# Flamingo block with four gated layers on one core: the last stage's token rows in fixed regions per expert, routed and sent group by group beside the attention

## The chip, the cores and the metric

One NeuronCore of a Trainium2 chip runs the whole block in one launch. The metric is the device time of that launch in microseconds (us), float32 in and out.

## What is computed

x is 2 x 1024 tokens of 256 values, the context 2 x 154 rows of 256. Four layers follow each other, each an attention on the context and a feed-forward part, all gated by tanh and added to x. Cut to the part that matters:

```python
x = x + tanh(g_ffn[2])   * L2_ffn(layernorm(x))               # 8 experts, the best one per token, 256 -> 1024 -> 256
x = x + tanh(g_xattn[3]) * L3_xattn(layernorm(x), ctx, ctx)   # single head, quantised weights, softmax over 154
x = x + tanh(g_ffn[3])   * L3_ffn(layernorm(x))

def L3_ffn(x, router_w, router_bias, gate_w, up_w, down_w, sgate_w, sup_w, sdown_w):
    scores = softmax(x @ router_w.T + router_bias)            # 32 experts
    topk_scores, topk_idx = top_k(scores, 4)
    topk_scores = topk_scores / topk_scores.sum(-1)
    h = silu(einsum('nd,ehd->neh', x, gate_w)) * einsum('nd,ehd->neh', x, up_w)
    sel = take(einsum('neh,edh->ned', h, down_w), topk_idx)
    out = (sel * topk_scores[..., None]).sum(1)
    return out + silu(x @ sgate_w.T) * (x @ sup_w.T) @ sdown_w.T   # the shared expert, 512 wide
```

## The kernel before

Tokens lie on the 128 partitions, 16 tiles of 128 (T), in four groups of four tiles (G = 4, GT = 4). Each engine has one program written out in order; they meet at semaphores. The stages are numbered 0 to 7: even ones are the attentions, odd ones the feed-forward parts. The change touches three of them and the filling of a buffer at the start.

Stage 5 (the 8 experts): the router gives each token a slot in a buffer xs5 in HBM, sorted by expert and padded to whole tiles of 128 (NT2 = 24 tiles). POOL scatters the 16 tiles of rows with indirect DMAs (scatter_gpsimd), the tile loop (expert_tiles_tensor, _scalar, _vector, _sync) loads a tile, multiplies it with its expert's weights and stores it to ys5 in the same order, and after the loop POOL gathers 16 tiles back with indirect DMAs (gather_gpsimd, L1130). combine_parts (L1138) adds a group to x_tok and starts its layer norm.

Stage 6 (single head): single_context_* turns the context into keys and values (L1150 to L1216). single_* then walks the four groups: ScalarE normalises (L1424), PE transposes (L1413), ScalarE copies (L1419), PE makes scores (L1229), VectorE adds the bias and takes the maximum, ScalarE takes the exponential, PE transposes it (L1244, L1249), ScalarE and VectorE (L1311) copy it, PE multiplies with the values (L1257, L1258), VectorE adds to x_tok (L1318). The scores of group g + 1 are made ahead of the rest of group g; a norm's small steps (L1344 to L1382) are put between other work of VectorE.

Stage 7: when all groups are through stage 6, route_tensor, route_scalar and route_vector take them one by one: norm, transposes, logits (L573), top 8 and their index (L614, L617), a 0/1 mark per expert (L621, L628), running sums over the tiles (L634). When all 16 tiles are marked, PE counts ranks (L580, L582), VectorE turns counts into tiles per expert and start tiles (L640 to L651), and a slot is start * 128 + rank (L655 to L663). shares_vector makes the four weights of each token. POOL then sends 64 tiles of rows (16 tiles x 4 choices, 268 values a row: the token and 12 extras) to xs7 (L686), a buffer of 96 tiles sorted by expert. Meanwhile shared_* computes the shared expert for three of the groups: per group four hidden steps of eight matmuls (L717, ScalarE's tanh L747, VectorE's L761 and L765), and an output of 32 matmuls (L727) with its addition (L755). quads_* then handles the 96 tiles four at a time, 24 quads: SP loads a quad (L774), PE transposes (L809), multiplies (L816, L833), VectorE selects the token and weight of each row, and POOL sends the rows to ys7 (L955). The last group of the shared expert and the combination (L965) follow.

The order inside the shared expert and the waits of its first step:

```python
pe.wait_ge(*slots_ready.at(7, 1))
pe.wait_ge(*expert_ready.at(7, 1))
pe.wait_ge(*logits_read.at(7, G))
for k in range(4 * groups[0], 4 * groups[-1] + 4):
    hidden(k)
    if k % 4 == 0 and k // 4 - 1 in groups:
        down(k // 4 - 1)
```

SP fills xs5 and xs7 with zeros at the start (L2427, L2429), after the loads of stages 0 to 3 and ahead of those of stage 2's attention, which wait for stage 0.

## Time and profile before

| | us |
|---|---|
| median of 3 runs (lowest, highest) | 1704.92 (1700.68, 1713.27) |
| the profiled execution | 1705.23 |
| its span, first to last instruction | 1703.5 |

| engine | busy us | share of the span |
|---|---|---|
| PE matmul | 1372.4 | 81% |
| PE weight load | 769.7 | 45% |
| VectorE | 755.6 | 44% |
| ScalarE | 439.3 | 26% |
| GpSimd (POOL) | 287.6 | 17% |

The engines' times are those of one profiled execution; PE is TensorE, DVE is VectorE, ACT is ScalarE, SP is SyncE, a name with q is an engine's instruction queue. A line L765 is line 765 of the kernel. In a row of the timeline stand start, length, engine, line, operation, output and inputs, the number of instructions, and in brackets how long the engine had been idle and what ended that. TensorE's granted clock is given as a share of full speed: 1.0 is the 2.4 GHz level, 0.5 the 1.2 GHz level.

### The profile page before, as it was taken

The page shows a single profiled execution, that of the slowest core. Times are in us where ns is not written, and L with a number is a line of the kernel's source. Part 1 is how long each engine was busy: PE and PEld are TensorE (multiplying, and loading weights), DVE is VectorE, ACT ScalarE, POOL GpSimd, SP SyncE. Part 2 cuts the span into 40 slices and gives each one's busy share as a digit, 9 for nine tenths or more (in the row PEclk, how much of TensorE's full clock was granted, in tenths as well). Part 3 has the DMA queues.
Part 4 walks back from the last instruction along what each step waited for, and adds up shares of the span by engine and source line. Part 5 has one row for each costly group of instructions (what it writes and reads, how often), then busy time and mean ns, then how long its engine had stood idle before and what let it go on. Part 6 is the DMA issues. An engine that isn't in the chain of part 4 may idle for free.

```text
span 1703.5 us, 18737 instructions
## 1 busy us (share of the span) xinstructions
PE 1372.4 (81%) x6041; PEld 769.7 (45%) x6042; DVE 755.6 (44%) x2011; ACT 439.3 (26%) x837; POOL 287.6 (17%) x300
## 2 busy tenths in 40 slices
PE   5999999999736799999988299997578605888883
PEld 3433334334323344444445267765346303677762
DVE  6363472381476235555644112212545402345446
ACT  2212212121142234444433033331223000223220
POOL 2200110010022000000000300002300472154550
PEclk9899999999967689999988599998765757999997
DMA  9600000000010000000003901111072131144436
GB/s 323 208 1 0 0 0 0 0 0 0 1 50 1 1 1 1 1 1 1 27 1 122 331 28 31 32 36 57 25 243 92 62 110 61 52 142 136 134 112 252
DMA packets 82953, 113.86 MB, mean 67 GB/s; under 512 B 7376, under 2 KB 71504, under 8 KB 82768
## 3 DMA queue, kind: packets, MB, share of 16 engines
q1 hardware_dynamic: 73680, 87.54, 15.9%
q0 software_dynamic: 9216, 25.57, 4.2%
q8 instruction: 34, 0.56, 0.1%
q14 instruction: 23, 0.19, 0.0%
HBM read 68.07 MB, written 45.02 MB: 66 GB/s over the span
## 4 chain that ended last, share of the span: by engine, by line
PE 70%; DVE 12%; issue 8%; ACT 4%; another core or an unknown queue 2%; DMA 1%; POOL 1%; SPq 1%; DVEq 0%; ACTq 0%; POOLq 0%
PE psum L1605 16%; PE psum L816 5%; PE psum L1030 5%; PE psum L1014 5%; PE psum L1773 5%; PE psum L717 4%; PE psum L1829 2%; DVE arena L2343 2%; PE psum L1759 2%; PE psum L1806 2%; PE psum L573 2%; PE psum L1562 2%; PE psum L1853 2%; PE psum L1596 2%
## 5 line engine op out<-in xcount | busy, mean ns | idle before, releaser
L1605 PE MATMUL psum<-arena 128*128 128x512 f32 (+1 forms) x576 | 294.0, 639 | 0.3
L1605 PEld LDWEIGHTS psum<-arena 128*128 128x128 f32 (+1 forms) x576 | 96.9, 193 | 165.1 <-issue 162.4
L2343 DVE TENSOR_REDUCE arena<-psum 128x4 f32<-128x616 f32 x128 | 102.0, 797 | 127.3 <-PE psum L1773 126.0
L1773 PE MATMUL psum<-arena 32*128 32x308 f32 x512 | 112.7, 519 | 24.2 <-DVE arena L2343 22.9
L955 POOL DMA_INDIRECT ys<-xnT,arena x96 | 92.2, 961 | 151.5 <-DVE xnT L921 128.2
L1939 ACT ACTIVATE arena<-psum,arena 128x512 f32<-128x512 f32 x72 | 49.1, 686 | 234.1 <-PE psum L1605 224.8
L816 PE MATMUL psum<-arena,xn 128*128 x384 | 89.2, 385 | 24.3 <-ACT xn L866 13.4
L2053 ACT ACTIVATE arena<-psum 128x2048 f32<-128x2048 f32 x40 | 75.0, 1875 | 76.7 <-PE psum L1810 59.7
L1030 PE MATMUL psum<-arena,xn 128*128 x384 | 88.6, 385 | 2.0 <-ACT xn L1076 2.0
L1014 PE MATMUL psum<-arena,side 128*128 x192 | 88.5, 604 | 1.0 <-ACT side L1069 0.6
L816 PEld LDWEIGHTS psum<-arena,xn 128*128 128x128 f32 x384 | 71.0, 190 | 38.5 <-issue 29.8
L717 PE MATMUL psum<-xnT,side 128*128 128x512 f32 x64 | 35.1, 710 | 65.4 <-issue 62.5
L1773 PEld LDWEIGHTS psum<-arena 32*128 32x128 f32 x512 | 42.2, 201 | 92.4 <-DVE arena L2343 61.3
L1095 DVE COPY xn<-psum 128x1024 f32<-128x1024 f32 x24 | 29.4, 1225 | 119.3 <-PE psum L1014 119.3
L1443 POOL TENSOR_TENSOR arena<-arena 128x1024 f32<-128x1024 f32 x15 | 28.3, 1893 | 298.3 <-DVE arena L2192 279.0
L686 POOL DMA_INDIRECT xs<-xn,arena x64 | 61.5, 961 | 101.7 <-DVE xn L707 82.5
L1030 PEld LDWEIGHTS psum<-arena,xn 128*128 128x128 f32 x384 | 72.3, 193 | 11.9 <-issue 2.8
L1512 POOL TENSOR_TENSOR x_tok<-x_tok,add_row 128x1024 f32<-128x1024 f32 x16 | 37.7, 2364 | 228.6 <-ACT xn L1424 157.1
L1076 ACT ACTIVATE xn<-psum,side 128x128 f32<-128x128 f32 x192 | 52.3, 384 | 86.8 <-PE psum L1023 86.8
L2176 DVE SCALAR_TENSOR_TENSOR arena<-arena 128x512 f32<-128x512 f32 x24 | 16.5, 688 | 117.3 <-ACT arena L1939 117.3
L1806 PE MATMUL psum<-arena 32*128 32x512 f32 x256 | 53.2, 667 | 1.9 <-ACT arena L2053 1.9
L717 PEld LDWEIGHTS psum<-xnT,side 128*128 128x128 f32 x64 | 14.4, 231 | 84.8 <-issue 81.1
(374 smaller groups left out, 2207.9 us busy)
## 6 DMA issues: line engine op xcount, KB each, us to landing
arena<-in_W SPq DMA_DIRECT2D x16, 1024.0 KB
xs<-zeros SPq DMA_DIRECT2D x1, 12864.0 KB, 53.9
xn<-xs SPq DMA_DIRECT2D x24, 536.0 KB
arena<-in_gate_up SPq DMA_DIRECT2D x4, 2048.0 KB, 15.0
arena<-ys SPq DMA_DIRECT2D x4, 2048.0 KB, 14.7
arena<-in_down SPq DMA_DIRECT2D x4, 1024.0 KB, 14.9
xs<-zeros SPq DMA_DIRECT2D x1, 3072.0 KB, 15.3
side<-xs SPq DMA_DIRECT2D x24, 128.0 KB
```

The source lines that it names most:

```text
L686: pool.indirect_dma_start(xs, bass.IndirectOffsetOnAxis(r["slot_i"][:, n, k:k + 1].bitcast(U32), 0), xn[:, n // GT, n % GT, 0:xs.shape[1]] ...
L717: ins = pe.matmul(bank[2 * (k % 2) + j], w[:, c, h * P:(h + 1) * P], place(7, g)[:, c], start=(c == 0), stop=(c == C - 1))
L816: ins = pe.matmul(bank[2 + t // 2][:, (t % 2) * 2 * F4:(t % 2 + 1) * 2 * F4], qinT[:, u, c, t * P:(t + 1) * P], arena[:, bass.ds(e * (C * ...
L955: pool.indirect_dma_start(ys7, bass.IndirectOffsetOnAxis(row_i[:, u, t:t + 1].bitcast(U32), 0), qout[:, u, t * D:(t + 1) * D], None).then_ ...
L1014: ins = pe.matmul(bank[2 + h], xinT[:, u, c * P:(c + 1) * P], W1[:, e, c * F2 + h * 512:c * F2 + h * 512 + 512] if isinstance(e, int) else ...
L1030: ins = pe.matmul(bank[6 + u][:, 0:D], hact[:, u, k * P:(k + 1) * P], arena[:, bass.ds(e * (8 * D) + (E2 * C * F2 + k * D), D)], start=(k ...
L1076: ins = act.activation(hact[:, u, k * P:(k + 1) * P], bank[4 + k // 4][:, k % 4 * P:(k % 4 + 1) * P], ACT.Relu, bias=b1col[:, bass.ds(e * ...
L1605: ins = pe.matmul(bank[dict(hn=4, r=5, z=6, xn=7)[k]][:], lhs[:, cols], r, start=(start and n == 0), stop=(stop and n == len(w) - 1))
L1773: ins = pe.matmul(bank[4 + i][:, 0:2 * M].rearrange("p (h m) -> p h m", h=2), qhT[rows, n % 3, c, t * P:(t + 1) * P], keys[rows, l, c, b, ...
L1806: pe.matmul(bank[j], keys[rows, l, r // 2, b, r % 2, 0:P], qhT[rows, n % 3, r // 2], start=True, stop=False, tile_position=(32 * j, 0))
L2053: act.activation(e_rest if r == 4 else e_head[:, r % 2], psum[:, 0:4], ACT.Exp, scale=HD ** -0.5).then_inc(weighed, 1)
L2343: dve.tensor_reduce(neg[:, n % 2, t, 2 * pair:2 * pair + 2, 2 * c:2 * c + 2], psum[:, 4:6, 0:2 * M].rearrange("p b (h m) -> p b h m", h=2) ...
```

## The change

1. xs7 becomes a region of 16 tiles for each of the 32 experts, and one spare tile of zeros: 513 tiles in place of 96, filled with zeros at the start in nine DMAs. A slot is expert * 2048 + rank, which needs no counts of the other groups. rows_vector works out, for the 96 tiles of the quad loop, the first row of each in the regions; SP reads it and loads each of a quad's four tiles by a DMA of its own.
2. Routing goes by groups: while group g is in stage 6, group g - 1 gets its norm, transposes (turn_late, copy_late), logits, marks (hot_vector), ranks and slots (slots_vector), and POOL scatters its 16 tiles of rows (scatter7_gpsimd). Group 3 follows inside the shared expert, by the functions in `then`, as do counts and tiles per expert. The shared expert no longer waits for all slots but for those of three groups.
3. Buffers move for it: the transposed groups 1 and 2 lie in the last quarter of the down weights' place, so that quarter (1 MB) is loaded after the twelfth hidden step. The router's weights are loaded with stage 5's.
4. Stage 5: rows carry their slot and token number, the tile loop's output goes to HBM in token order by one indirect DMA a tile (scatter_out5_gpsimd), with a selection on VectorE (select), and four plain loads (combined5_sync) take the place of the 16 gathers.

The core of the diff:

```diff
+REGION = T
+SPARE = E4 * REGION
...
-        tanh_s = xq[:].rearrange("p u n -> p (u n)").bitcast(F32).rearrange("p (u n) -> p u n", u=2)
...
+        tanh_s = arena[:, 28672:29696].rearrange("p (u n) -> p u n", u=2)
+        xnT7 = [xq[:].rearrange("p u n -> p (u n)").bitcast(F32).rearrange("p (c n) -> p c n", c=C)] + [
+            region.rearrange("p (c n) -> p c n", c=C)
+            for region in (arena[:, TAIL - 2048:TAIL - 1024], arena[:, TAIL - 1024:TAIL], side[:, 3200:4224])]
...
-        ys5 = nc.dram_tensor("ys5", (NT2 * P, D), F32, kind="Internal").ap()
-        xs7 = nc.dram_tensor("xs7", (NT4 * P, DX), F32, kind="Internal").ap()
+        xs5 = nc.dram_tensor("xs5", (NT2 * P, D5), F32, kind="Internal").ap()
+        ys5 = nc.dram_tensor("ys5", (1 + T * P + NT2 * P, D), F32, kind="Internal").ap()
+        xs7 = nc.dram_tensor("xs7", ((SPARE + 1) * P, DX), F32, kind="Internal").ap()
...
+        def turn_late(pe, s, g):
+            i, b = late_turns[s, g], late_bank(s, g)
+            pe.wait_ge(*xn_ready.at(s, g + 1))
+            for c in range(C):
+                if b == 0 and i:
+                    pe.wait_ge(*xnT_ready.at(6, (i - 1) * C + c + 1))
+                for t in range(GT):
+                    ins = pe.transpose(bank[b + c][:, t * P:(t + 1) * P], xn[:, g, t, c * P:(c + 1) * P], ident[:])
+                ins.then_inc(turned.sem, 1)
+        def copy_late(act, s, g):
+            i, b = late_turns[s, g], late_bank(s, g)
+            for c in range(C):
+                act.wait_ge(*turned.at(6, i * C + c + 1))
+                act.activation(place(s, g)[:, c], bank[b + c][:], ACT.Copy).then_inc(xnT_ready.sem, 1)
...
+        def logits_tensor(pe, g):
+            pe.wait_ge(wr7_loaded, 2 * 16)
+            pe.wait_ge(*xnT_ready.at(6, (late_turns[7, g] + 1) * C))
+            for t in range(GT):
+                for c in range(C):
+                    ins = pe.matmul(logit_bank[:, t * E4:(t + 1) * E4], place(7, g)[:, c, t * P:(t + 1) * P], wr7[:, c],
+                                    start=(c == 0), stop=(c == C - 1))
+            ins.then_inc(logits_done.sem, 1)
+        def ranks_tensor(pe, g):
+            r = route[7]
+            pe.wait_ge(*hot_ready.at(7, g + 1))
+            pe.wait_ge(*earlier_ready.at(7, 1 + GT * (g + 1)))
+            if g == G - 1:
+                pe.matmul(bank[5][0:E4, 128:129], r["earlier"][:, T], ones_bf[:, 0:1], start=True, stop=True)
+            for t in range(GT):
+                dst = rank_bank[:, t * E4:(t + 1) * E4]
+                pe.matmul(dst, before[:], r["any_hot"][:, t], start=True, stop=False)
+                ins = pe.matmul(dst, ones_bf[:], r["earlier"][:, g * GT + t], start=False, stop=True)
+            ins.then_inc(ranks_done.sem, 1)
...
+        def hot_vector(dve, ch, g):
+            r = route[7]
+            if g == 0:
+                dve.wait_ge(route_consts, 7)
+                dve.memset(r["earlier"][:, 0], 0.0).then_inc(earlier_ready.sem, 1)
+            dve.wait_ge(*logits_done.at(7, g + 1))
+            dve.tensor_tensor(r["logits"], logit_bank.rearrange("p (t e) -> p t e", t=GT),
+                              br7.unsqueeze(1).broadcast_to([P, GT, E4]), ALU.add).then_inc(logits_read.sem, 1)
+            dve.wait_ge(*logits_read.at(7, g + 1))
+            for t in range(GT):
+                ch.step(dve.max(r["top"][:, t], r["logits"][:, t]))
+            ch.settle()
+            for t in range(GT):
+                ch.step(dve.max_index(r["index"][:, t], r["top"][:, t], r["logits"][:, t]))
+            if g:
+                dve.wait_ge(shares_exp, g)
+            dve.tensor_tensor(r["share"], r["top"][:, :, 0:K4], r["top"][:, :, 0:1].broadcast_to([P, GT, K4]),
+                              ALU.subtract).then_inc(shares_shifted, 1)
+            ch.settle()
+            ch.step(dve.tensor_copy(r["index_f"], r["index"][:, :, 0:K4]))
+            ch.settle()
+            if g:
+                dve.wait_ge(*ranks_done.at(7, g))
+            ch.step(dve.tensor_tensor(r["hot"].rearrange("p t k e -> p (t k) e"),
+                                      iota_e[:].unsqueeze(1).broadcast_to([P, GT * K4, E4]),
+                                      r["index_f"].rearrange("p t k -> p (t k)").unsqueeze(2).broadcast_to([P, GT * K4, E4]),
+                                      ALU.is_equal))
+            ch.settle()
+            with nc.allow_low_precision(reason="sums of zeros and ones"):
+                dve.tensor_reduce(r["any_hot"], r["hot"].rearrange("p t k e -> p t e k"), AX.X, ALU.add).then_inc(hot_ready.sem, 1)
+            dve.wait_ge(*hot_ready.at(7, g + 1))
+            for t in range(GT):
+                n = g * GT + t
+                dve.wait_ge(*earlier_ready.at(7, n + 1))
+                dve.tensor_tensor(r["earlier"][:, n + 1], r["earlier"][:, n], r["any_hot"][:, t],
+                                  ALU.add).then_inc(earlier_ready.sem, 1)
...
+        def slots_vector(dve, ch, g):
+            r = route[7]
+            dve.wait_ge(shares_exp, g + 1)
+            ch.step(dve.tensor_reduce(r["total"], r["share"], AX.X, ALU.add))
+            ch.settle()
+            ch.step(dve.reciprocal(r["total"], r["total"]))
+            ch.settle()
+            ch.step(dve.tensor_scalar(r["total"], r["total"], gain(7), None, ALU.mult))
+            ch.settle()
+            ch.step(dve.tensor_tensor(xn[:, g, :, D + K4:D + 2 * K4], r["share"],
+                                      r["total"].unsqueeze(2).broadcast_to([P, GT, K4]), ALU.mult))
+            dve.wait_ge(*ranks_done.at(7, g + 1))
+            ch.step(dve.scalar_tensor_tensor(r["place"], iota_e[:].unsqueeze(1).broadcast_to([P, GT, E4]), float(REGION * P),
+                                             rank_bank.rearrange("p (t e) -> p t e", t=GT), ALU.mult, ALU.add))
+            slot = r["slot"][:, g * GT:(g + 1) * GT]
+            for k in range(0, K4, 2):
+                ch.settle()
+                ch.step(dve.tensor_tensor(r["picked"], r["hot"][:, :, k:k + 2],
+                                          r["place"].unsqueeze(2).broadcast_to([P, GT, 2, E4]), ALU.mult))
+                ch.settle()
+                ch.step(dve.tensor_reduce(slot[:, :, k:k + 2], r["picked"], AX.X, ALU.add))
+            ch.settle()
+            ch.step(dve.tensor_copy(xn[:, g, :, D:D + K4], slot))
+            ch.settle()
+            dve.tensor_copy(r["slot_i"][:, g * GT:(g + 1) * GT], slot).then_inc(slots_ready.sem, 1)
...
+        def rows_vector(dve, ch):
+            r = route[7]
+            dve.wait_ge(*expert_done.at(7, 1))
+            ch.step(dve.tensor_tensor(rowid, bank[5][:, 256:256 + NT4], iota_n[:, 0:NT4], ALU.add))
+            ch.step(dve.tensor_scalar(r["expert_f"][0:1], bank[4][0:1, 256:256 + NT4], float(E4 - 1), None, ALU.min))
+            ch.settle()
+            ch.step(dve.tensor_scalar(rowid, rowid, float(SPARE), float(P), ALU.min, ALU.mult))
+            quad = r["expert_f"][0:1].rearrange("p (q t) -> p q t", t=4)
+            for t in range(2, -1, -1):
+                ch.step(dve.scalar_tensor_tensor(quad[:, :, t], quad[:, :, t + 1], float(E4), quad[:, :, t], ALU.mult, ALU.add))
+                ch.settle()
+            ch.step(dve.tensor_copy(first_row[0:1], rowid[0:1]))
+            ch.step(dve.tensor_copy(r["expert"][0:1, 0:NQ], quad[:, :, 0]))
+            ch.settle()
+            dve.tensor_scalar(rowid, rowid, pcol[:], None, ALU.add).then_inc(expert_ready.sem, 1)
...
+        def scatter7_gpsimd(pool, g):
+            pool.wait_ge(*slots_ready.at(7, g + 1))
+            for t in range(GT):
+                n = g * GT + t
+                for k in range(K4):
+                    pool.indirect_dma_start(xs7, bass.IndirectOffsetOnAxis(r7["slot_i"][:, n, k:k + 1].bitcast(U32), 0),
+                                            xn[:, g, t], None).then_inc(scattered.sem, 16)
...
-            pe.wait_ge(*expert_ready.at(7, 1))
-            pe.wait_ge(*logits_read.at(7, G))
+            pe.wait_ge(ws_loaded, 3 * 16)
+            pe.wait_ge(*xnT_ready.at(6, (late_turns[7, G - 1]) * C))
+            pe.wait_ge(scores_read6, 2 * G)
+            pe.wait_ge(*logits_read.at(7, G - 1))
+            pe.wait_ge(*slots_ready.at(7, G - 1))
             for k in range(4 * groups[0], 4 * groups[-1] + 4):
                 hidden(k)
+                if k in then:
+                    then[k]()
...
             def load(q, u):
-                sp.dma_start(qin[:, u], xs7[bass.ds(q * 4 * P, 4 * P), :].rearrange("(t p) d -> p t d", p=P)
-                             ).then_inc(in_loaded[u].sem, 16)
+                for t in range(4):
+                    row = sp.value_load(first_row[0:1, bass.ds(4 * q + t, 1)], min_val=0, max_val=SPARE * P)
+                    sp.dma_start(qin[:, u, t], xs7[bass.ds(row, P), :]).then_inc(in_loaded[u].sem, 16)
+            sp.wait_ge(*expert_ready.at(7, 1))
             sp.wait_ge(*scattered.at(7, T * K4 * 16))
             load(0, 0)
             load(1, 1)
+            sp.wait_ge(shared_done, 4 * (G - 1))
+            sp.dma_start(DW[:, 24:32], d["down"][24 * F4:32 * F4].rearrange("(e p) n -> p e n", p=P)).then_inc(w7_loaded, 16)
...
+        def combined5_sync(sp):
+            for u in range(2):
+                sp.wait_ge(*sent[u].at(5, NT2 // 2 * 16))
+            for g in range(G):
+                sp.dma_start(gathered5[:, g * GT:(g + 1) * GT],
+                             ys5[1 + g * GN:1 + (g + 1) * GN].rearrange("(t p) d -> p t d", p=P)).then_inc(gathered_in[g].sem, 16)
...
+            def select(i, u, turn):
+                one = slice(i, i + 1) if isinstance(i, int) else bass.ds(i, 1)
+                if not isinstance(turn, int) or turn:
+                    dve.wait_ge(*out_ready.at(5, i - 1))
+                dve.wait_ge(*in_loaded[u].at(5, 16 * turn + 16))
+                dve.scalar_tensor_tensor(token_row5[:, u:u + 1], xin[:, u, D:D + 1], rowid5[:, one], xin[:, u, D + 1:D + 2],
+                                         ALU.is_equal, ALU.mult).then_inc(chosen.sem, 1)
+                dve.wait_ge(*chosen.at(5, i + 1))
+                dve.scalar_tensor_tensor(no_token5[:, u:u + 1], token_row5[:, u:u + 1], 0.0, unused_row5[:, one],
+                                         ALU.is_equal, ALU.mult).then_inc(selected5, 1)
...
-            for n in range(T):
-                pool.indirect_dma_start(gathered5[:, n], None, ys5,
-                                        bass.IndirectOffsetOnAxis(route[5]["slot_i"][:, n, 0:1].bitcast(U32), 0)
-                                        ).then_inc(gathered5_in[n // GT], 16)
+        def scatter_out5_gpsimd(pool):
+            for i in range(NT2):
+                u = i % 2
+                pool.wait_ge(*out_ready.at(5, i + 1))
+                pool.indirect_dma_start(ys5, bass.IndirectOffsetOnAxis(row_i5[:, u:u + 1].bitcast(U32), 0), yout[:, u],
+                                        None).then_inc(sent[u].sem, 16)
...
+                if g:
+                    turn_late(pe, 7, g - 1)
                 pe.wait_ge(main_copied6, g + 1)
                 pe.wait_ge(rest_copied6, g + 1)
+                if g:
+                    logits_tensor(pe, g - 1)
                 if g:
                     pe.wait_ge(*x_done.at(6, g))
                 for t in range(GT):
                     ins = pe.matmul(dst, probs6R[0:MR, u, t * P:(t + 1) * P], vals6R[0:MR, b], start=False, stop=True)
                     if t % 2:
                         ins.then_inc(pv_done6, 1)
+                if g:
+                    ranks_tensor(pe, g - 1)
...
+                if g:
+                    normalise_scalar(act, 7, g - 1)
                 act.wait_ge(turned6, 2 * g + 1)
                 if g >= 2:
                     act.wait_ge(pv_done6, 2 * (g - 1))
                 act.activation(probs6T[:, u], bank[4], ACT.Copy).then_inc(main_copied6, 1)
+                if g:
+                    copy_late(act, 7, g - 1)
+                    share_scalar(act, g - 1)
...
+                run(norm)
                 if g + 1 < G:
                     scores(g + 1)
-                run(finish(g), norm)
-                run(norm)
+                finishing = finish(g)
+                run(itertools.islice(finishing, 3))
+                if g:
+                    hot_vector(dve, ch, g - 1)
+                run(finishing)
+                if g:
+                    slots_vector(dve, ch, g - 1)
...
+                for n, first in enumerate(range(0, SPARE + 1, 64)):
+                    many = min(64, SPARE + 1 - first)
+                    sp.dma_start(xs7[first * P:(first + many) * P].rearrange("(t p) d -> p t d", p=P),
+                                 zeros[:].unsqueeze(1).broadcast_to([P, many, DX])).then_inc(zeroed, 16)
...
-                route_tensor(pe, 7, wr7, (ws_loaded, 5 * 16), free=lambda: pe.wait_ge(*x_done.at(6, G)))
-                shared_tensor(pe, range(G - 1))
+                shared_tensor(pe, range(G - 1), {
+                    1: lambda: (turn_late(pe, 7, G - 1), logits_tensor(pe, G - 1)),
+                    2: lambda: ranks_tensor(pe, G - 1),
+                    3: lambda: start_tensor(pe),
+                    4: lambda: tiles_tensor(pe)})
...
-                route_vector(dve, ch, 7, br7)
-                shares_vector(dve, ch)
-                shared_vector(dve, ch, range(G - 1))
+                shared_vector(dve, ch, range(G - 1), {
+                    1: lambda: (hot_vector(dve, ch, G - 1), slots_vector(dve, ch, G - 1), tiles_vector(dve, ch)),
+                    2: lambda: passed_vector(dve, ch),
+                    4: lambda: rows_vector(dve, ch)})
```

## Rows read from the trace of the kernel before

**Rows 1.** Busy time by stretches: window, length, busy us (count), granted clock, DMA share, GB/s.

```profile
80.00:484.00 404.00, 372.45 (x907) 141.74 (x905) 206.98 (x362) 80.55 (x124) 42.33 (x25) 0.95 0.00 0
...
1240.00:1295.00 55.00, 42.35 (x121) 25.53 (x121) 26.90 (x116) 13.19 (x39) 2.56 (x2) 0.59 0.82 259
...
1335.00:1464.00 129.00, 68.95 (x191) 38.36 (x192) 21.03 (x36) 7.31 (x13) 61.91 (x66) 0.74 0.22 77
...
1464.00:1656.00 192.00, 163.24 (x867) 139.37 (x865) 90.03 (x265) 54.24 (x96) 87.35 (x91) 1.00 0.39 125
```

**Rows 2.** The chain that ended last, from 1334 to 1465: start, us, what.

```profile
1334.80 20.07 PE psum L717 x40
...
1361.78 3.43 PE psum L717 x8
1365.21 55.09 issue
...
1457.30 7.17 PE psum L727 x32
```

**Rows 3.** Timeline around the stop in the shared expert.

```profile
1337.56 1.00 POOL L686 DMA_INDIRECT xs<-xn,arena  x1 [82.47 <-DVE xn L707]
...
1417.30 0.96 POOL L686 DMA_INDIRECT xs<-xn,arena  x1 [0.30 <-issue]
...
1419.56 0.69 DVE L765 SCALAR_TENSOR_TENSOR arena<-xq,psum 128x512 f32<-128x512 f32 x1 [63.33 <-remote]
```

**Rows 4.** Timeline at the end of stage 5's gathers.

```profile
1195.03 1.91 PE L1167 MATMUL psum<-arena,ctxT 128*26 128x256 f32 x8
...
1199.05 1.20 PE L1178 MATMUL psum<-arena 128*128 128x308 f32 x4
...
1199.53 0.95 POOL L1130 DMA_INDIRECT side<-ys,xq  x1 [0.30 <-issue]
...
1203.31 0.68 DVE L1211 COPY arena<-psum 26x512 f32<-26x512 f32 x1 [7.08 <-remote]
...
1205.08 1.65 DVE L1138 SCALAR_TENSOR_TENSOR x_tok<-side,tanh_g,x_tok 128x256 f32<-128x256 f32 x4
```

**Rows 5.** Timeline of the single-head attention, from its second group on.

```profile
1240.33 1.97 PE L1413 MATMUL psum<-ident,xn 128*128 128x128 f32 x8
...
1253.18 1.19 PE L1257 MATMUL psum<-arena 128*128 128x256 f32 x2 [4.51 <-issue]
...
1262.35 1.97 PE L1413 MATMUL psum<-ident,xn 128*128 128x128 f32 x8
...
1294.27 0.48 DVE L1318 SCALAR_TENSOR_TENSOR x_tok<-psum,arena,x_tok 128x256 f32<-128x256 f32 x1
...
1295.39 1.40 DVE L1365 BATCH_NORM_STATS2 stats<-x_tok 128x6 f32<-128x256 f32 x4
...
1296.12 0.60 ACT L1419 ACTIVATE xnT<-psum 128x512 f32<-128x512 f32 x1 [12.40 <-PE psum L1413]
...
1299.49 0.16 DVE L1382 COPY scale_ln<-nwt 128x4 f32<-128x4 f32 x1
```

**Rows 6.** Timeline of the routing: one group's logits and marks, and the slots.

```profile
1297.47 2.06 ACT L1424 ACTIVATE xn<-x_tok,shift_ln,scale_ln 128x256 f32<-128x256 f32 x4
...
1309.76 3.62 PE L573 MATMUL psum<-side,arena 128*128 128x32 f32 x16 [0.69 <-ACT arena L1419]
...
1313.42 0.29 DVE L610 TENSOR_TENSOR arena<-psum,side 128x128 f32<-128x128 f32 x1 [1.46 <-PE psum L573]
...
1317.01 1.01 DVE L634 TENSOR_TENSOR arena<-arena 128x32 bf16<-128x32 bf16 x4
...
1327.68 0.69 DVE L659 TENSOR_TENSOR arena<-arena 128x512 f32<-128x512 bf16 x1
```

**Rows 7.** DMA issues: what, queue, count, KB each, us to landing.

```profile
xs<-zeros SPq DMA_DIRECT2D x1, 12864.0 KB, 53.9
```

**Rows 8.** Timeline of one expert tile of stage 5, VectorE.

```profile
1093.89 1.23 DVE L1095 COPY xn<-psum 128x1024 f32<-128x1024 f32 x1 [3.78 <-PE psum L1014]
```

312 lines of the change are left out of this document (169 added, 143 removed).

## The prediction

> **What bounds the kernel now.** I read the page first (PE is busy for 81% of the span, but the slices show it at 7 and lower in the last third), then the busy time by stretches, then the chain that ended last, and last the timeline around each hole of the chain. The stretches [rows 1] are to be read by PE's busy time against their length and by the granted clock: the expert quads (1464 to 1656) run at clock 1.00 with PE busy 163 of 192 us, while the attention (1240 to 1295) was granted 0.59 and the 129 us from 1335 on have PE busy for only 69. The chain says what those 129 us are [rows 2]: 20 us of shared-expert matmuls, 55.1 us in which PE issues nothing, and the rest of the shared expert, which ends at 1457.30 + 7.17 = 1464.5. So about 170 us lie between the end of the single-head attention and the first quad, and the matmuls of three shared groups in them are 62 us of work (12 hidden steps of 3.43 and 3 outputs of about 6.9, at the 2.4 GHz level). That is what the change can take.
>
> Why PE stood still is in [rows 3]. POOL issues its 64 scatters from 1337.56 on, one each 1.266 us, the last at 1417.30. The output matmuls of the first shared group (L727) are through at 1361.78, where the chain goes on with a hidden step [rows 2]; VectorE's L765, which waits only for them, starts at 1419.56, 57.8 us later and 1.3 us after the last scatter's issue. The same is seen once more, smaller, in the gathers of stage 5 [rows 4]: L1167 ends at 1196.94, VectorE's L1211 starts at 1203.31, 2.8 us after the last gather's issue ended. So a long run of indirect DMAs held back what PE had finished, in both runs that lie over working engines, and not before some 12 of them were out (the 16 gathers began 15 steps of 1.266 before 1199.53, at 1180.5). The rows call the releaser remote; the cause they don't show.
>
> **Stage 5 and the zeroing: near nothing.** The fill of the row buffer for the last stage grows from 96 to 513 tiles. The 12,864 KB took 53.9 us [rows 7], so 513 tiles take 288 us; begun within the first 20 us it is done by 310, and no DMA ran from 80 to 484 (share 0.00) [rows 1]; SP has nothing to load before. Priced at 0; were that cover gone, the attention weights of stage 2, next in SP's queue, would wait for the excess. In the 24 expert tiles SP loses its stores, POOL gains one indirect DMA a tile (1.27 of 8 us), VectorE two one-column operations and an add, 0.5 us together; VectorE idles 3.78 us in each tile before L1095 alone [rows 8], so these are hidden. SP's load now also waits for the selection two tiles back, over 11 us ahead of its use. The 16 gathers, 20 us of POOL, become four plain loads, and with them goes the hold at 1196.9 [rows 4]. VectorE would go on with L1211 at 1197.0 and, after PE's L1178 (ends 1200.3), reach its first combination at 1200.9 in place of 1205.08: **-4.2 us**.
>
> **Single-head attention: longer.** Groups 0 to 2 of the routing move in here. Per group PE gets 8 transposes (1.97 us), 16 logit matmuls (3.62) and 8 small rank matmuls (0.3), ScalarE a normalisation of 2.06 and two copies of 0.60 (1.3), VectorE the top-k part (L610 at 1313.42 to the last running sum at 1318.02: 4.6, with the share's subtraction 4.8) and the slots (four share operations 1.07, place 0.3, four operations at half the 512 elements of L659, 1.6, two copies 0.4: 3.4) [rows 5, 6]. All of it is at the 1.2 GHz level, as the stretch was granted 0.59 [rows 1]. The period of group 1 was 1240.33 to 1262.35. PE waited in it until 1253.18 for VectorE's copy; the transposes fit there, the logits come behind: **+3.6**. In groups 2 and 3 the new order makes one chain: last addition 0.9, slots of the group before 3.4, its norm 4.2 (1295.39 to 1299.65), ScalarE 2.1, transposes 2.0, copies 1.3, logits 3.6, the PV matmuls 9.2 (1253.18 to 1262.35): 26.7. Twice that, 53.4, stands in place of 31.2 (1262.35 to the end of the last PV matmul at 1293.5, just ahead of the last additions): **+22.2** [rows 5]. Bounds: if the fuller PE is granted 2.4 GHz, PV and logits halve and some 15 us come back; nothing lower.
>
> **Routing gap: gone but for one group's slots.** From VectorE's last addition (ends 1294.75) to the first shared matmul (1334.80) were 40.0 us; now PE waits for the slots of group 2, 3.4: **-36.6** [rows 2, 5].
>
> **Shared expert.** Its three groups take 61.9 us of PE. Put between them are group 3's transposes and logits (2.8 at the fast level), and PE waits where VectorE does routing: for ScalarE's copies 1.4, for the top-k before the ranks 2.2, for the tile counts and the next product 3.5, before the last output 2.1 as before: 9.2. Together 73.9, in place of 129.3 (1334.80 to 1464.1): **-55.4**. POOL's last burst starts some 20 us into this stage and takes 16 x 1.266 = 20.2, so the rows are all out by 42, with 32 us to spare before the first quad. The last quarter of the down weights, 1 MB, is now loaded after the twelfth hidden step, under an output of 6.9 and a wait of 2.1; at the zeroing's rate (12,864 KB in 53.9 us [rows 7]) it takes 4.3 us, so 5 to 7 with its start. Quads: four loads of a quad in place of one; SP issues one in about 0.5 us and has 7.9 per quad, priced 0. Tail unchanged.
>
> Sum: -4.2 + 3.6 + 22.2 - 36.6 - 55.4 = -70.4. The profiled execution took 1705.23 (span 1703.5), the median is 1704.92, so one stands for the other: 1634.5 without any hold.
>
> **The holds.** The 64 scatters now come in four bursts of 20.2 us, three with PE and VectorE handing work to each other and the third and fourth nearly back to back. What the trace bounds: nothing (as in the quads, where four DMAs in 7.9 us hold nobody for long), or all of every burst, 81 us. It is nearest to the gathers, also 16 DMAs: onset 16.3 us after the first, 6.4 us late in all. Four times that is 25; about half falls where VectorE isn't waited for. I take **+12**, and forecast **1646**.
>
> The Trainium skill ("SBUF — State Buffer", Who interferes with whom) has only one place where VectorE and GpSimd get into each other's way, a port pair that VectorE takes for operations with two SBUF inputs or in a two-port mode. L765 and L1211 read PSUM and at most one SBUF operand, so by that rule they would never be held and the time would be 1634; the row of 57.8 us speaks against it, and the measurement decides.
>
> **Rivals.**
> A, no hold, perhaps with PE at the higher clock in the attention: 1634, down to 1619. For it: bursts are 16 long, onset came after 12 or more. Against: 2 of 2 long runs held.
> B, the bursts hold much more: from the middle of each burst to its end and 2.8 us on, 13 us x 4 = 52: 1686. For it: in the long run the hold covered 58 of 82 us. Against: the gathers' 6.4.
> C, slower than before: each burst holds PE's results for its whole length, so that burst, selection and the next burst follow in series: 4 x 20.2 = 81 on 1634 gives 1715. It decides from 17.6 us held per burst on. Against it: 12 scatters went by without delay in both runs [rows 3, 4].
> D, the change doesn't do its main thing: the quads don't start when the shared groups end, because the weights' last quarter or the four loads are late. Each would cost at most its own length, 7 us, and 1 us per quad if the loads took over 7.9 us of SP: 1634 + 7 + 24 = 1665. The issues of 0.5 us speak against it.
>
> **How the numbers follow.** Forecast (holds of 5 to 25 in all) 0.5, A 0.18, B 0.17, C 0.07, D 0.08. The range leaves out C and the ends of A and B: 1618 to 1692. A measurement of this kernel tells about 1% from no change; faster than 1688 is the forecast, A, D and most of B, 0.85; within 1% the rest of B and part of C, 0.08; slower 0.07.
>
> **What would show it.** The first shared matmul (L717 before) near 1319 in place of 1334.8; the first quad near 1393 to 1405 in place of 1464; no PE gap over 20 us between them; the attention at 105 us in place of 84, clock still near 0.6; the four bursts of 16 apart by more than their length except the last two; a zeroing that ends near 310. Wrong would be: a VectorE wait with remote as releaser in each burst (B, C), a quad period over 8 us (D), or a slot iteration longer than its 130 us while the zeroing runs.

## The result, and the profile after

| | before | changed |
|---|---|---|
| median of 4 runs (lowest, highest), us | 1706.79 (1700.68, 1713.27) | 1653.06 (1651.77, 1657.03) |
| profiled span, us | 1703.5 | 1655.1 |

The ratio is 0.9694, with a 95% interval of 0.9664 to 0.9725: 3.1% faster. Forecast were 1646 and a range of 1618 to 1692. The spans differ by 48.4 us, the medians by 53.7; the profiled execution is the slowest of its four (1657.03).

The working below goes by stretches between the starts of certain instructions in the timelines, since these can be told in every variant:

| stretch, us | before | changed |
|---|---|---|
| last output matmul of stage 5 to VectorE's first combination (L1138, now L1328) | 28.0 | 22.8 |
| to the first score matmul of stage 6 (L1229, now L1419) | 10.8 | 10.9 |
| attention and routing: to the first shared matmul (L717, now L878) | 118.9 | 110.9 |
| shared expert: to the first quad's matmul (L816, now L990) | 131.5 | 93.2 |
| quads: to the last hidden matmul of the last quad | 181.9 | 185.5 |
| tail | 55.4 | 55.4 |

Up to the end of stage 5 the two are 0.6 us apart. Busy time by stretches of the changed kernel, columns as in [rows 1]:

```profile
1234.60:1321.00 86.40, 59.63 (x217) 40.46 (x216) 51.45 (x217) 20.99 (x56) 33.25 (x34) 0.56 0.60 203
...
1321.00:1414.00 93.00, 76.25 (x236) 43.83 (x236) 34.08 (x100) 11.26 (x21) 30.92 (x33) 0.88 0.22 71
...
1414.00:1600.00 186.00, 159.11 (x837) 136.49 (x838) 84.77 (x252) 51.50 (x93) 82.42 (x86) 0.99 0.42 125
```

The shared stretch has 76 us of PE's work in 93, where [rows 1] had 69 in 129. The chain that ended last says where the other 17 are (start, us, what); "another core or an unknown queue" is its name for a wait whose releaser the profile doesn't show (the timeline's "remote"); no other core runs here:

```profile
1321.04 9.34 PE psum L878 x16
...
1332.44 9.80 another core or an unknown queue
1342.26 0.29 DVE arena L645
...
1358.78 12.46 another core or an unknown queue
1371.26 0.70 DVE arena L933
1371.96 0.04 issue
1372.01 12.26 PE psum L878 x24
1384.27 6.91 PE psum L888 x32
...
1403.61 8.86 PE psum L888 x32
...
1414.26 1.77 PE psum L990 x7
```

The 55.1 us of [rows 2] have become two holes of 9.8 and 12.5. The timeline shows that they are of the kind of [rows 3]:

```profile
1199.33 1.26 DVE L1328 SCALAR_TENSOR_TENSOR x_tok<-side,tanh_g,x_tok 128x256 f32<-128x256 f32 x3
...
1287.81 1.66 DVE L1523 SCALAR_TENSOR_TENSOR x_tok<-psum,arena,x_tok 128x256 f32<-128x256 f32 x4 [3.50 <-remote]
...
1332.23 1.84 PE L606 MATMUL psum<-side 128*128 128x32 f32 x15
...
1340.11 0.96 POOL L868 DMA_INDIRECT xs<-xn,arena  x1 [0.30 <-issue]
1342.26 0.29 DVE L645 TENSOR_TENSOR arena<-psum,side 128x128 f32<-128x128 f32 x1 [9.82 <-remote]
...
1357.57 7.17 PE L888 MATMUL psum<-side,arena 128*128 128x256 f32 x32
...
1364.58 3.60 PE L878 MATMUL psum<-arena,side 128*128 128x512 f32 x8
...
1369.10 0.96 POOL L868 DMA_INDIRECT xs<-xn,arena  x1 [0.30 <-issue]
...
1371.26 0.69 DVE L933 SCALAR_TENSOR_TENSOR arena<-arena,psum 128x512 f32<-128x512 f32 x1 [12.54 <-remote]
```

POOL sends in four bursts of 16, from 1265.0, 1292.9, 1321.2 and 1350.1, one DMA each 1.265 us. VectorE's L645 waits for the logits (L606), through at 1334.1 and 13 us into the third burst; it starts at 1342.26, 8.2 us late and 1.2 us after the burst's last DMA. L933 waits for the output matmuls (L888), through at 1364.7, and starts 6.5 us late, again 1.2 us after the end of a burst. I call such a late start a hold. The first burst has two: L645 starts at 1278.5, 1.7 us after its matmuls and in the middle of the burst, and L1523 at 1287.8, 2.9 us after the last DMA. In the second burst no wait names remote. Two waits of the quads (who, for whom, us in all, times, longest):

```profile
ACT xn L1040 <- remote: 16.3, 12, 2.0
...
PE psum L983 <- DMA xn<-xs: 2.1, 1, 2.1
```

And the fill among the DMA issues, its eight large ones:

```profile
xs<-zeros SPq DMA_DIRECT2D x8, 8576.0 KB, 60.0
```

### The profile page after: what moved, and what is told of

Its sections match the earlier page's. It is cut to its first block, busy times and chain, and to the rows that moved or that the text cites. A ratio compares the mean times of both kernels' runs of the same rounds, so it can differ in the third digit from the quotient of the medians.

```text
span 1655.1 us, 19515 instructions
## 1 busy us (share of the span) xinstructions
PE 1370.3 (83%) x6042; PEld 768.6 (46%) x6043; DVE 774.8 (47%) x2121; ACT 438.6 (27%) x840; POOL 295.4 (18%) x310
## 4 chain that ended last, share of the span: by engine, by line
PE 69%; DVE 14%; issue 6%; ACT 5%; another core or an unknown queue 3%; DMA 2%; POOL 1%; SPq 1%; DVEq 0%; ACTq 0%; POOLq 0%
PE psum L1816 16%; PE psum L1201 5%; PE psum L1185 5%; PE psum L1984 5%; PE psum L990 5%; PE psum L878 3%; PE psum L2040 2%; DVE arena L2555 2%; PE psum L2017 2%; PE psum L1773 2%; PE psum L1970 2%; PE psum L2064 2%; PE psum L1807 2%; PE psum L888 1%
## 5 line engine op out<-in xcount | busy, mean ns | idle before, releaser
L1816 PE MATMUL psum<-arena 128*128 128x512 f32 (+1 forms) x576 | 289.3, 630 | 0.3
L990 PE MATMUL psum<-arena,xn 128*128 x384 | 89.1, 385 | 24.1 <-issue 13.1
L990 PEld LDWEIGHTS psum<-arena,xn 128*128 128x128 f32 x384 | 71.0, 190 | 38.1 <-issue 29.4
L1321 POOL DMA_INDIRECT ys<-side,xq x24 | 23.0, 959 | 183.8 <-DVE side L1284 183.8
L1069 DVE SCALAR_TENSOR_TENSOR arena<-arena,psum 128x512 f32<-128x512 f32 x24 | 16.5, 688 | 76.9 <-issue 50.0
```

The source lines that it names most:

```text
L990: ins = pe.matmul(bank[2 + t // 2][:, (t % 2) * 2 * F4:(t % 2 + 1) * 2 * F4], qinT[:, u, c, t * P:(t + 1) * P], arena[:, bass.ds(e * (C * ...
L1816: ins = pe.matmul(bank[dict(hn=4, r=5, z=6, xn=7)[k]][:], lhs[:, cols], r, start=(start and n == 0), stop=(stop and n == len(w) - 1))
```

## The experiments

Three theories: **S**, an unbroken run of POOL's indirect DMAs holds back what PE signals, until about a microsecond after the run (the first burst above doesn't fit this end); **F**, the delay is PE's own or belongs to these places in the code; **W**, there is no hold and the sum left out work. The kernels ran in three sets, each on a chip of its own; the kernel before took 1708.0 us on the first, 1708.7 on the second and 1666.8 on the third. Ratios are to the kernel before on the same chip. The changed kernel itself ran only in the first comparison (on which chip is not known) and not in these sets; its row below has the ratio of that comparison.

### First chip: does the hold go with the DMAs?

**One choice of four.** `for k in range(K4)` in POOL's burst becomes

```diff
-                for k in range(K4):
+                for k in range(1):
```

> The changed kernel with only the first of each token's four choices sent: four bursts of 4 indirect DMAs in place of four of 16. Left out: three quarters of the routed rows (their outputs are zeros; the row buffer of the outputs is zeroed at the start for that, 8 MB more under the first stage). All engine work, the number of expert tiles and every wait stay. Theory S (a long unbroken run of indirect DMAs on POOL holds back what PE signals; 4 in a row are too few): the holds seen in the changed kernel's trace (about 10 us in the third burst, 12.5 in the fourth, 2 to 4 in the first two) go, VectorE's waits with remote as releaser shrink below 2 us each, the shared stage is 74 to 78 us in place of 91, time 1629 to 1636. Theory F (PE's delay belongs to its own instruction stream or to these places in the code, not to the DMAs): the same holes at the same instructions, 1650 to 1655. Theory W (no hold; my sum for the shared stage left out real work or waits of the routing): 1648 to 1655, with the same 91 us.

**Paced by four.**

```diff
                 for k in range(K4):
                     pool.indirect_dma_start(xs7, ..., xn[:, g, t], None).then_inc(scattered.sem, 16)
+                pool.wait_ge(*scattered.at(7, (n + 1) * K4 * 16))
```

> The changed kernel with all 64 scatters, but POOL waits after every four until these have landed. Nothing is left out. Theory S (an unbroken run is what holds): each burst becomes four pieces of 5 us with gaps of 1 to 2 us, 26 to 30 us long; the last ends by about 1380, still ahead of the first quad; the holds go: 1630 to 1638, first quad at 1396 to 1400 in place of 1414. Rival Q (every indirect DMA of POOL costs PE's signals its share, however they are spaced): as much is held as before or more, since the bursts are longer: 1650 to 1660. Theory F (PE's own instruction stream): 1650 to 1655.

**Plain stores from SyncE.**

```diff
-                    pool.indirect_dma_start(xs7, bass.IndirectOffsetOnAxis(...), xn[:, g, t], None)
+                    sp.dma_start(xs7[(n * K4 + k) * P:(n * K4 + k + 1) * P, :], xn[:, n // GT, n % GT])
```

> The changed kernel with the 64 indirect scatters replaced by 64 plain stores of the same tiles (128 rows of 268 numbers) from SyncE's queue, after the same slots. Left out: the rows go to fixed places, so the experts see wrong rows (output buffer zeroed at the start as in the run with one choice); engine work and tile count stay. Theory S (it is POOL's indirect DMAs): no hold, 1629 to 1636. Rival D (it is the transfers' traffic, 137 KB each, whoever issues them): holds of the size seen before, 1645 to 1655. Theory F: 1650 to 1655.

**The kernel before, paced by four.** The same added line, in its one run of 64.

> The kernel before, with POOL waiting after every four of its 64 scatters of the last stage until they have landed. Nothing is left out. Theory S: VectorE's wait of 57.8 us at L765 goes, the three shared groups end near 1334.8 + 62 + 10 = 1407; the scatters take 81 + 16 x 1.5 to 2 = 105 to 113 us and end at 1443 to 1451, and they, not the shared expert, now set the first quad, at 1446 to 1454 in place of 1466: 1685 to 1694 in place of 1705. Theories F and Q (pacing changes nothing in what is held): the hold lasts as long as the scatters do, shared expert to about 1490, 1725 to 1735.

| | median us | ratio, 95% | attention | shared | quads |
|---|---|---|---|---|---|
| changed | 1653.1 | 0.969, 0.966 to 0.972 | 110.9 | 93.2 | 185.5 |
| one choice | 1645.4 | 0.964, 0.958 to 0.970 | 105.7 | 77.1 | 188.2 |
| paced by four | 1642.0 | 0.965, 0.959 to 0.971 | 105.8 | 77.2 | 186.7 |
| stores from SyncE | 1636.4 | 0.960, 0.956 to 0.964 | 105.8 | 77.0 | 186.0 |
| before, paced | 1693.0 | 0.991, 0.988 to 0.995 | 121.2 | 113.8 | 184.8 |

The two stages that the bursts lie over are alike in all three variants of the changed kernel, 5.1 and 16.1 us shorter than in the changed kernel itself. The engines' work and its order are unchanged in them, which speaks against F and W, and pacing sends all 64, which speaks against the rival by which every indirect DMA costs its share. It counts only if this chip holds at all, since the unpaced bursts were not run on it. That shows in the kernel before with its scatters paced (the gathers, left unpaced, below) and is settled on the second chip. The paced kernel's timeline at the place of the second hole:

```profile
1343.07 7.17 PE L889 MATMUL psum<-side,arena 128*128 128x256 f32 x32
...
1344.03 0.96 POOL L868 DMA_INDIRECT xs<-xn,arena  x1 [1.74 <-DMA xs<-xn,arena]
...
1347.81 0.96 POOL L868 DMA_INDIRECT xs<-xn,arena  x1 [0.30 <-issue]
...
1350.28 0.69 DVE L934 SCALAR_TENSOR_TENSOR arena<-arena,psum 128x512 f32<-128x512 f32 x1 [6.06 <-PE psum L889]
```

POOL pauses 1.74 us after four, and VectorE starts at the end of the output matmuls, with PE as the releaser. The medians say less than the stretches. They lie above what S gave for one choice and for pacing (1629 to 1636, 1630 to 1638), and the intervals of the paced and the changed kernel overlap; the stages before this one differ between executions (the first output matmul of stage 5 starts between 982.5 and 998.7 in the profiles), more than what is looked for. Of the spans, 1655.1 and 1636.0 are 19.1 apart, which is 5.1 + 16.1, less 1.2 in the quads and 0.9 elsewhere.

In the paced kernel before, the chain ends with the scatters, as expected:

```profile
1439.76 2.47 DMA xs<-xn,arena
1442.25 3.65 DMA xn<-xs
...
1448.84 3.35 PE psum L818 x7
```

The 57.8 us of [rows 3] are gone, and 15 us of time with them; the rest of that wait was covered by the scatters' own length. Its gathers were left unpaced, and their hold stayed, on the copy of [rows 4]:

```profile
1200.45 0.68 DVE L1213 COPY arena<-psum 26x512 f32<-26x512 f32 x1 [6.42 <-remote]
```

### Second chip: which DMAs, how many, and what else

**Plain stores from POOL.** As with SyncE, but `pool.dma_start`.

> The changed kernel with its 64 indirect scatters issued by POOL as 64 plain stores of the same tiles to fixed rows, in the same unpaced bursts. Left out: the right places of the rows, as in the run with SyncE's stores (output buffer zeroed at the start). It tells what in POOL's bursts holds PE's signals. Theory S1 (any DMA that POOL issues in an unbroken run): the holds of the changed kernel are there at similar instructions if the bursts are as long (1.27 us a DMA), shared stage 85 to 92 us, 1645 to 1655. Theory S2 (only the indirect ones): no hold, shared stage 75 to 77 us as in the three runs before, 1632 to 1640.

**Quads send one tile of four** (on top of the pacing).

```diff
-                for t in range(4):
+                for t in range(1):
                     pool.indirect_dma_start(ys7, ..., qout[:, u, t * D:(t + 1) * D], None).then_inc(sent[u].sem, 16)
```

> The paced kernel (POOL waits after every four scatters) and, in the quads, POOL sends only the first of a quad's four output tiles. Left out: three quarters of the output rows (zeros in their place). In the quads ACT's second input copy waits for PE's transposes with remote as releaser, 2.1 us in most quads. Theory S extended (four DMAs in a row hold too, from about 3.5 us after the first until 1 us after the last): that wait goes, and a quad's period of 7.9 to 8 us falls by 1 to 2 us, 1600 to 1622. Rival P (the late signal is PE's own, its transposes are only signalled with the matmuls behind them): the wait stays, 1636 to 1642 as the paced kernel.

**Quads send two pairs** (on top of the pacing).

```diff
+                    if t == 1:
+                        pool.wait_ge(*sent[u].at(7, 64 * (q // 2) + 32))
```

> The paced kernel with each quad's four output scatters sent as two pairs, POOL waiting between them until the first pair has landed. Nothing is left out. Theory S extended: two in a row are too few to hold, a quad's DMAs then take about 7 us of its 7.9, the remote waits of ACT's second input copy shrink from 2.1 us, and the time is 1605 to 1630. If POOL becomes the bound instead (its last DMA later than VectorE's next copy): 1640 to 1655. Rival P: 1636 to 1642.

**Gathers of stage 5 put back.**

```diff
-            for g in range(G):
-                sp.dma_start(gathered5[:, g * GT:(g + 1) * GT], ys5[...].rearrange(...))
+                for n in range(T):
+                    pool.indirect_dma_start(gathered5[:, n], None, ys5, bass.IndirectOffsetOnAxis(rows5g[:, n:n + 1]...))
```

> The changed kernel with one part undone: the outputs of stage 5 are read back by 16 indirect gathers on POOL, as before, in place of SyncE's four plain loads. Nothing is left out (the output buffer is zeroed at the start, 5 MB more). My term: the hold at the end of the gathers comes back, VectorE's context copy is released about 6 us late, first combination 4.2 us later than with the loads: 1657 in place of 1653. Rival: the hold was of no account there and the loads only start the combination earlier: within 1 us of the changed kernel.

| | median us | ratio, 95% | stage 5's end | attention | shared | quads |
|---|---|---|---|---|---|---|
| stores from POOL | 1639.9 | 0.960, 0.953 to 0.967 | 23.1 | 105.5 | 77.2 | 186.4 |
| quads one | 1633.3 | 0.956, 0.949 to 0.963 | 23.0 | 105.9 | 77.3 | 185.0 |
| quads pairs | 1641.6 | 0.959, 0.953 to 0.965 | 23.0 | 106.1 | 76.9 | 187.4 |
| gathers back | 1666.8 | 0.975, 0.967 to 0.983 | 25.8 | 110.6 | 91.0 | 185.8 |

Only the last has unpaced indirect bursts, and only it shows the holds (waits of VectorE with remote as releaser: 6.7 and 5.6 us in the first burst, 9.4 in the third, 11.0 in the fourth). With the pairs, whose bursts are paced, this is the comparison on one chip that the first set lacked: 91.0 against 76.9 us. Its 16 gathers add their own:

```profile
1206.03 1.20 PE L1367 MATMUL psum<-arena 128*128 128x308 f32 x4
...
1209.72 0.95 POOL L2732 DMA_INDIRECT side<-ys,rows5g  x1 [0.30 <-issue]
1210.05 0.48 DVE L1405 COPY arena<-psum 128x308 f32<-128x308 f32 x1 [3.05 <-remote]
```

The first combination comes 2.9 us later than with the loads, where I expected 4.2; in the kernel before the same kind of wait was 7.08 [rows 4]. The median missed my 1657 by 10 us; of the 10.7 us between this profile's span (1665.8) and that of the changed kernel, 8.2 lie before stage 5's first output matmul, so the stretches decide here too.

S has the end of the hold wrong, as the fourth burst of this run shows:

```profile
1367.20 7.17 PE L890 MATMUL psum<-side,arena 128*128 128x256 f32 x32
...
1379.37 0.69 DVE L935 SCALAR_TENSOR_TENSOR arena<-arena,psum 128x512 f32<-128x512 f32 x1 [11.02 <-remote]
...
1380.06 0.96 POOL L870 DMA_INDIRECT xs<-xn,arena  x1 [0.30 <-issue]
```

VectorE starts 5.0 us after the matmuls that it waits for, but with one more DMA of the run to come; ScalarE, which waits for the next matmuls (through at 1377.8), starts only at 1383.7, 2.7 us after the run. The hold goes with the run, its end isn't set by the run's end alone.

POOL's plain stores hold nobody, but they don't settle whether the kind or the length counts: 16 of them pass in 8.6 us (542 ns busy each, against 959), and in the indirect bursts of 16 nothing was late before 10 us either.

In the quads the hold exists as well on the first two chips: ScalarE's second input copy was released by "remote", 18 or 19 times in the variants with one choice and with pacing. Without three of the four DMAs, or in pairs, no such wait is left; yet the quads take 185.0 and 187.4 us against 186.7 in the paced kernel. The 1600 to 1622 and 1605 to 1630 that I had expected did not come. The chain of the paced kernel puts 23% of the quads' time down to that wait, but at most 1.7 us was to be had there; that PE had its own matmuls to do meanwhile fits, and wasn't tried by itself. It also leaves a gap in S: in the quads runs of four hold, 3 us apart and beside SyncE's loads, and in the paced bursts, 1.7 us apart, they don't.

### Third chip: the order undone, the two prices of zero, a last version

**Everything sent late.**

```diff
-            pool.wait_ge(*slots_ready.at(7, g + 1))
+            pool.wait_ge(*slots_ready.at(7, G))
```

> The changed kernel with one part undone: every group is still routed where the change put it, but POOL sends nothing until the last group's slots are known, so that all 64 scatters go in one run from about 1340 us on. Nothing is left out. Theory S: the run ends at about 1340 + 64 x 1.266 = 1421, PE's signals are held from 10 to 20 us into it until a microsecond or two after its end, and most of the shared expert comes after 1422 (about 45 to 55 of its 77 us): first quad at 1465 to 1480, time 1700 to 1720: no gain is left over the kernel before. Rival E (early routing is what pays, the sending could be late; the hold is short as in the changed kernel, 5 to 16 us): the quads wait only for the rows, first quad at 1425 to 1435, 1665 to 1675.

**The fill twice**: the eight large DMAs and the small one once more, after the first nine.

> The changed kernel with the fill of the row buffer done twice, 1026 tiles in place of 513. Nothing is left out. My term: the fill is hidden under the first stage, where nothing else is to be loaded before 484 us; the double fill ends at about 500 at the rate of the changed kernel (250 us for one), so at most 16 us of it show, and the stages up to 484 are as long as before: 1653 to 1668; if SyncE issues the next weights as its queue comes free and nobody waits for them, 1653. Rival Z (the fill's traffic slows the slot iterations): the first 484 us grow by over 3 us, and in the changed kernel by half of that.

**One load per quad.**

```diff
-                for t in range(4):
-                    row = sp.value_load(first_row[0:1, bass.ds(4 * q + t, 1)], ...)
-                    sp.dma_start(qin[:, u, t], xs7[bass.ds(row, P), :])
+                row = sp.value_load(first_row[0:1, bass.ds(4 * q, 1)], ...)
+                sp.dma_start(qin[:, u], xs7[bass.ds(row, 4 * P), :].rearrange("(t p) d -> p t d", p=P))
```

> The changed kernel with each quad's rows loaded by one DMA of 536 KB, as before, in place of four of 134 KB with a row number each. Left out: three of a quad's four tiles come from the wrong region (the output buffer is zeroed at the start). The quads from first to last hidden matmul took 181.9 us before and 185.4 to 188.2 in the changed kernel and its variants: what is disputed is whether the four loads cost that, which I had priced at 0. If they do: PE's waits for the loads of the third and fourth quad (0.5 and 2.4 us) go, the quads take 182 to 183 us, and the time is 2 to 4 us less, 1649 to 1651. If not (the first two selections, late in VectorE's order, or the last weights' load of 1 MB ahead in SyncE's queue, set those loads): 185 to 186 us again, 1653.

**Paced, spread, early selections.**

```diff
+            select(0, 0, 0)
+            select(1, 1, 0)
             hidden(0, 0)
-            select(0, 0, 0)
             hidden(1, 1)
-            select(1, 1, 0)
...
-                    1: lambda: (hot_vector(dve, ch, G - 1), slots_vector(dve, ch, G - 1), tiles_vector(dve, ch)),
-                    2: lambda: passed_vector(dve, ch),
-                    4: lambda: rows_vector(dve, ch)})
+                    1: lambda: hot_vector(dve, ch, G - 1),
+                    3: lambda: (slots_vector(dve, ch, G - 1), tiles_vector(dve, ch)),
+                    5: lambda: passed_vector(dve, ch),
+                    7: lambda: rows_vector(dve, ch)})
```

> A version that should beat both: the changed kernel with paced scatters (a wait after every four), the first two quads' selections ahead of VectorE's first hidden steps, so that the loads of the third and fourth quad go out earlier, and the last group's routing spread over more hidden steps (slots and counts after the fourth, not the second; the two small products after the fifth and seventh). Nothing is left out. Theory: shared stage 77 us less 2 to 4 (PE's short waits for VectorE), quads 186 less 3: 1630 to 1637 against 1636 to 1642 of the paced kernel. Rival: VectorE is loaded as before and the waits only move: 1636 to 1642; if POOL's last burst, now some 7 us later, sets the first quad: 1642 to 1648.

| | median us | ratio, 95% | attention | shared | quads |
|---|---|---|---|---|---|
| before | 1666.8 | | | | |
| all late | 1680.8 | 1.009, 1.004 to 1.013 | 105.3 | 120.6 | 187.6 |
| fill twice | 1637.4 | 0.982, 0.973 to 0.992 | 105.6 | 77.6 | 185.6 |
| one load | 1633.1 | 0.979, 0.971 to 0.988 | 105.7 | 77.3 | 183.7 |
| spread | 1647.7 | 0.986, 0.977 to 0.995 | 105.8 | 80.5 | 183.7 |

The first surprise is the kernel before: 13 runs from 1658.6 to 1681.8, none near the 1698 to 1724 of its 20 runs on the first two chips. The second is that "fill twice" and "one load" have the bursts of the changed kernel, unpaced, and the stretches of the paced one. In the timeline of "fill twice", the fourth burst (and no wait in the whole profile names remote as its releaser):

```profile
1344.72 5.77 PE L888 MATMUL psum<-side,arena 128*128 128x256 f32 x26
...
1349.88 0.96 POOL L868 DMA_INDIRECT xs<-xn,arena  x1 [0.30 <-issue]
...
1350.53 0.69 DVE L933 SCALAR_TENSOR_TENSOR arena<-arena,psum 128x512 f32<-128x512 f32 x1 [6.06 <-PE psum L888]
...
1356.20 0.96 POOL L868 DMA_INDIRECT xs<-xn,arena  x1 [0.30 <-issue]
```

In the changed kernel this instruction started 6.5 us after its matmuls, here at once, in the middle of the burst. Three of the four kernels here send unpaced, and none is held, "all late" with its 64 in a row among them. The changed kernel itself wasn't run here; these three send unpaced like it, and each differs from it in another place. So a long run of indirect DMAs isn't enough for the hold: it needs something that differs between the chips, or between what else went on there. What that is, no run tells. It would also account for the faster kernel before, of which there is no trace from this chip: paced on the first chip, its first quad came 9.1 us after its last scatter's start (1439.76 to 1448.84); the same from 1417.30 on [rows 3] gives 1426.4 in place of 1466.3, an estimate of 40 us for the measured 41.

"All late" therefore tested something else than I meant, the sending alone: the rows are what the quads wait for, and one thing more.

```profile
1414.13 2.44 DMA xs<-xn,arena
1425.71 5.38 DMA arena<-in_down
1431.14 1.98 PE psum L983 x8
1433.98 2.07 PE psum L990 x4
```

The last row lands at 1416.6; then SyncE takes 8.1 us to issue the first two quads' eight loads, and the last weights take 5.4, both queued behind the wait for the rows. Late sending costs 43.0 us in this stage (120.6 against 77.6) and the whole gain; early sending is what the change lives on, on this chip without any hold. My forecasts for it failed, S with 1700 to 1720 and the rival with 1665 to 1675, though the first quad, at 1434.0, is in the rival's range (1425 to 1435). The case of 64 late DMAs on a chip that holds wasn't tried.

The fill is free also when doubled: the stages up to stage 5's first output take 990.4 us against 989.5, and PE is busy for 372.43 us from 80 to 484 as in [rows 1], with the DMA share there at 1.02 in place of 0.00. One load for four takes 1.9 us off the quads; so do the early selections. The same two waits go in both: with four loads PE waits for the rows of the third and fourth quad (0.3 and 2.25 us in "fill twice"), since their load waits for a selection and then takes four issues. What stays over the kernel before is in the second quad: its 16 hidden matmuls take 5.40 us with one load (5.34 in "fill twice"), before they took 3.72, as 0.52 was granted from 1401.9 to 1405.4.

```profile
1401.93 5.40 PE L989 MATMUL psum<-arena,xn 128*128 x16 [0.84 <-issue]
```

The spread routing gains nothing (forecast were 1630 to 1637): its shared stage is 3.3 us longer than the paced one. That is seen in the granted clock, columns as above:

```profile
1323.31:1361.30 37.99, 32.89 (x107) 19.08 (x108) 17.71 (x68) 6.25 (x12) 21.56 (x23) 0.87 0.22 79
```

The paced kernel was granted 0.96 in its first 38 us and did its first 16 hidden matmuls in 8.5 us and its first outputs in 7.1, this one in 10.2 and 8.8. Nor did the waits shrink: PE still waits for VectorE's slots and counts, 3.2 us at one place. Whether the clock came of the new order or of the execution stays open: three of its four executions took 1646.5 to 1649.2 us at a mean granted clock of 0.881, the fourth 1632.2 at 0.894.

Of the versions that leave nothing out, only the pairs' interval (0.953 to 0.965) lies below that of the changed kernel (0.966 to 0.972), by a hair and across two comparisons. By the stretches, the changed kernel with pacing is the best where the hold occurs (21 us less over attention and shared expert than without). Where it doesn't, pacing cost nothing in the attention (105.8 in the spread kernel, 105.6 in "fill twice"); pacing alone wasn't run there.

## Why the prediction was right or wrong

The direction, the place and the two stretches that give the gain were right. The sum without holds, 1703.5 - 70.4 = 1633.1 us as a span, is near the paced kernel's 1636.0, in part by luck: against it the terms are off by -0.8 (end of stage 5), -2.3 (attention), +1.1 (shared expert) and +4.8 (quads). Step by step:

- **End of stage 5, -4.2.** 28.0 to 22.8, -5.2, of which the gathers put back return 2.9. The term is the size of one hold, and that differs between executions.
- **Attention and routing gap, +3.6 + 22.2 - 36.6 = -10.8.** -13.2 without hold (118.9 to 105.7). The period of group 1 was forecast as 25.6 and is 25.7; of the next two I said 26.7 each, they are 25.8 and, with the burst over it, 28.6 (25.9 in the paced kernel; start of L606 to start of L606). The clock stayed at 0.56, so the 15 us of the higher clock did not come. The first shared matmul starts at 1321.04, forecast 1319. The attention's "105 in place of 84" mixes two starts: from the first score matmul it was 78.8 us before (1215.91 to 1294.75), and 78.8 + 3.6 + 22.2 is 104.6.
- **Shared expert, -55.4.** -54.3 without hold (131.5 to 77.2), -38.3 with it.
- **Holds, +12.** This is the step that failed, by its size: 5.1 us in the attention and 16.1 in the shared expert, 21.2. I counted the gathers' 6.4 four times and struck half as lying where VectorE isn't waited for. The last two bursts alone gave 8.2 and 6.5 at instructions on the chain, since PE and VectorE hand work to and fro there in every microsecond. The clock was lower as well where PE stood: 0.80 granted from 1321 to 1357.5, 0.96 in the paced kernel. The low end of my bounds, no hold, is what the third chip has; one trace could not tell that.
- **Quads, 0.** 181.9 to 185.5. Of the 3.6 us, 2.8 are in one period, from the second quad's hidden matmuls to the third's: 10.62 us, before 7.82. PE waits 2.1 us there for the rows, and its transposes and output matmuls behind that wait take 1.67 and 3.03 us in place of 1.04 and 1.89, with 0.62 granted from 1427.5 to 1432. I had priced the four loads by SyncE's time per quad, at 0.5 us an issue; with its row number an issue takes 1.0 us, and the cost is at the start, where a load waits for a selection and PE waits for the load.
- **Fill, 0.** Right, also for the double fill. It ended at some 250 us, earlier than my 310, as it moved 313 to 337 GB/s by the slices of the page.

Of the rivals, A is what happens on the third chip. B (52 us held) and C (81) ask for more than the trace after has. D's two parts are there in small: 2 us for the loads, and in "all late" the weights' last quarter behind the rows. Of the signs of being wrong, VectorE's remote waits came in three of the four bursts, but that sign can't tell B from the forecast, which has holds too; by the price (21.2 us against 12 and 52) the forecast is the nearer one. A quad period over 8 us could tell nothing, since the periods went to and fro between 7.6 and 8.1 us in the kernel before as well.

The Trainium skill ("SBUF — State Buffer", Who interferes with whom) would have no hold at all. The measured 57.8, 8.2 and 6.5 us decide against it, and the 5.0 us on the second chip; on the third chip the traces agree with it, with no remote wait in four profiles. That the difference lies in the port pair which it names is not shown: L645 and L933 read PSUM, and where they aren't held they have the same operands.

## What to carry to other kernels

Break a long run of indirect DMAs that lies over engines handing work to each other: a wait after every four cost 1.7 to 2.0 us each in most places (up to 5.1 beside the weights' loads), was hidden in the changed kernel, and removed waits of up to 57.8 us. Send rows as soon as a part of them is routed, for the transfers' own length (1.265 us each) is the floor, held or not. A wait on the chain need not be worth its length: some two microseconds in most quads were on the chain, and their removal gave at most 1.7 us in all. Compare a change on more than one chip.
